# State part's products in parts of 64 output partitions, with the order of a group's work rearranged

## What is computed

```python
scores = einsum('bclhg,bcshg->bchls', Cc, Bc) * decay * dtT
Y_intra = einsum('bchls,bcshp->bclhp', scores, Xc)
w = exp(cum[:, :, -1:, :] - cum) * dtc
S = einsum('bcshg,bcshp->bchgp', Bc * w[..., None], Xc)
carry = dl[:, :, None, None] * carry + s              # state from chunk to chunk
Y_inter = einsum('bclhg,bchgp->bclhp', Cc * exp(cum)[..., None], Hprev)
y = rmsnorm((Y_intra + Y_inter + D_skip[:, None] * Xc) * silu(z), gnorm_w)
# feed-forward part, after the output product, a layernorm and the residual:
scores_xy, idx_xy = top_k(sim, 8)                     # best keys of 2 x 4 heads
w = silu((h . down_embed[chosen]) * softmax(scores))
out = silu(h @ W_up.T) @ W_down.T + sum(w * up_embed[chosen])
```

## Time and profile before

| | |
|---|---|
| runs | 2712.41, 2712.59, 2716.40 us |
| profiled execution | 2715.71 us, span of its trace 2714.0 us |
| busy: PE / DVE / POOL / ACT | 2644.7 / 2252.2 / 2132.0 / 1737.1 us |
| share of the span | 97% / 83% / 79% / 64% |
| mean granted TensorE clock | 0.992 of full |
| one pass in the loop | 81.67 us, the same in every pass to within 0.05 us |

### The profile page before, as it was taken

One profiled execution on the slowest core, in us unless ns is written; L12 is line 12 of the kernel. 1 busy time (PEld: TensorE's weight loads), 2 busy tenths in 40 slices (PEclk: granted clock), 3 DMA queues, 4 the chain that ended last, 5 costly groups with the idle time before them and its releaser, 6 DMA issues. The chain is left out here.

```text
span 2714.0 us, 50697 instructions
## 1 busy us (share of the span) xinstructions
PE 2644.7 (97%) x14888; PEld 2187.2 (81%) x14888; DVE 2252.2 (83%) x5390; ACT 1737.1 (64%) x3687; POOL 2132.0 (79%) x3127
## 2 busy tenths in 40 slices
PE   6899999999999999999999999999999999999988
PEld 5788887888888888887888887888887888887867
DVE  4688888898888898888988888988888888888864
ACT  5566666666666666666666666675666676666643
POOL 4478788888788888788888788888788888888863
PEclk8999999999999999999999999999999999999989
DMA  3000000000000000000000000000000000000000
GB/s 139 9 8 13 13 4 8 12 12 12 12 0 12 12 12 12 8 4 12 12 12 12 8 4 12 12 12 12 5 7 12 12 12 12 4 8 12 8 5 8
DMA packets 28856, 34.26 MB, mean 13 GB/s; under 512 B 2704, under 2 KB 27280, under 8 KB 28240
## 3 DMA queue, kind: packets, MB, share of 16 engines
q1 hardware_dynamic: 28816, 33.77, 3.9%
HBM read 25.37 MB, written 8.39 MB: 12 GB/s over the span
## 5 line engine op out<-in xcount | busy, mean ns | idle before, releaser
L1183 DVE SCALAR_TENSOR_TENSOR acc<-bank,cw,acc 128x253 f32<-128x253 f32 x1920 | 767.9, 471 | 168.4 <-ACT acc L834 168.3
L1539 PE MATMUL bank<-hT,w_in 128*128 128x256 f32 x2560 | 603.1, 381 | 8.7 <-DVE acc L1183 7.9
L1539 PEld LDWEIGHTS bank<-hT,w_in 128*128 128x128 f32 x2560 | 482.6, 191 | 114.2 <-issue 45.2
L642 POOL TENSOR_TENSOR Em<-ee 128x1024 f32<-128x1024 f32 x256 | 558.5, 2201 | 7.6 <-issue 7.6
L1338 DVE SCALAR_TENSOR_TENSOR Em<-Em,p 128x1024 f32<-128x1024 f32 x256 | 418.0, 1643 | 4.9 <-POOL Em L642 4.9
L969 ACT ACTIVATE Em<-Em,rden 128x1024 f32<-128x1024 f32 x256 | 292.6, 1144 | 139.2 <-DVE Em L1347 139.2
L834 ACT ACTIVATE acc<-bank,cb,cw 128x253 f32<-128x253 f32 x640 | 323.7, 559 | 0.0
L657 POOL TENSOR_TENSOR W<-W,Em 128x1024 f32<-128x1024 f32 x122 | 315.1, 2583 | 7.7 <-POOL ee L627 0.2
L1347 DVE TENSOR_TENSOR Em<-Em,products 128x1024 f32<-128x1024 f32 x252 | 305.4, 1212 | 3.3
L1725 PE MATMUL bank<-h2T,w_up 128*128 128x256 f32 x1024 | 242.1, 379 | 1.4 <-ACT hid L947 1.4
L1759 PE MATMUL bank<-w_ue,WT 128*128 128x256 f32 x1024 | 236.2, 384 | 4.9 <-ACT WT L979 4.9
(11 more groups left out here) (208 smaller groups left out, 5240.7 us busy)
## 6 DMA issues: line engine op xcount, KB each, us to landing
x_in<-x_dram SPq DMA_DIRECT2D x32, 256.0 KB, 2.7
x_res<-x_dram SPq DMA_DIRECT2D x32, 256.0 KB, 2.7
out_dram<-f SPq DMA_DIRECT2D x32, 256.0 KB, 2.2
w_in<-in_wT_dram SPq DMA_DIRECT2D x1, 1544.0 KB, 8.8
w_in<-in_wT_dram SPq DMA_DIRECT2D x1, 1024.0 KB, 5.2
w_up<-upT_dram SPq DMA_DIRECT2D x1, 1024.0 KB, 13.4
w_de<-down_eT_dram SPq DMA_DIRECT2D x1, 1024.0 KB, 15.4
w_down<-downT_dram SPq DMA_DIRECT2D x1, 1024.0 KB, 17.4
```

The source lines that it names most:

```text
L642: nc.gpsimd.tensor_tensor(Em[:, k], bc(ee[:, k, 0:XD], 2, KEYS), bc(ee[:, k, XD:XD + KEYS], 1, XD), ALU.mult).then_inc(E_done.sem, 1)
L1183: ins = V.scalar_tensor_tensor(acc[:, r, a, TAPS - 1:], ps[:, a * TOK + k:(a + 1) * TOK - TAPS + 1 + k], cw[:, t, k:k + 1], acc[:, r, a, T ...
L1539: last = mm(ring[j % 2][:, a * TOK:(a + 1) * TOK], w_in[:, k, at:at + P], hT[:, k, :], start=k == 0, stop=k == DK - 1)
```

## The change

The products of `mixer_Yi`, `mixer_S` and the intra-chunk part of `mixer_Yn` are issued as two products each, one for output partitions 0 to 63 and one for 64 to 127; `mixer_dt` is issued in four parts of 32. The number of f32 products in such a block goes from 8 to 16 (dt: 4 to 16) with the same streamed columns. Four waits are added (`mixer_parts` on `cum_sb`, `mixer_state` on `ecum_done`, `ffn_times` on `A_ps`, `ffn_A` on `h2T_sb`), and every engine's order is rearranged. These steps move from the end of a pass to the start of the next: on POOL `weigh(., 1, 0)`, `tail_root3`, `collect(., 0, 1)`; on ACT `mixer_square(., 1)`, `ffn_experts(., 0, 2)`; on DVE `ffn_times(., 0, 2)` and `(., 0, 3)`, `tail_sum`, `mixer_step(., 1)`. The same steps stand at the head of each engine's `ending`.

Indentation is cut; "..." marks what is left out. First TensorE:

```diff
@@ -1516,8 +1548,9 @@
         pe.wait_ge(Yn_read.sem, Yn_read.at(g - 1, CH - 1))
     for c in range(CH):
         for k in range(DK):
-            last = mm(yb[:, c * HEADS:(c + 1) * HEADS], hT[:, k, c * P:(c + 1) * P],
-                      w_in[:, k, INNER + XBC:], start=k == 0, stop=k == DK - 1)
+            for t in range(0, P, 32):
+                last = mm(yb[t:t + 32, c * HEADS:(c + 1) * HEADS], hT[:, k, c * P + t:c * P + t + 32],
+                          w_in[:, k, INNER + XBC:], start=k == 0, stop=k == DK - 1)
...
     for h in range(HEADS):
-        last = mm(ring[1 - c][:, h * HD:(h + 1) * HD],
-                  xbcT[:, INNER // P + HEADS + h, c * P:(c + 1) * P], H[:, h * HD:(h + 1) * HD],
-                  start=True, stop=True)
+        for t in (0, HALF):
+            last = mm(ring[1 - c][t:t + HALF, h * HD:(h + 1) * HD],
+                      xbcT[:, INNER // P + HEADS + h, c * P + t:c * P + t + HALF],
+                      H[:, h * HD:(h + 1) * HD], start=True, stop=True)
     last.then_inc(Yi_ps.sem, 1)
...
     pe.wait_ge(X_sb.sem, X_sb.at(g, c))
     for h in range(HEADS):
-        last = mm(ring[c][:, h * HD:(h + 1) * HD], Btok[:, h, :], Xw[:, h * HD:(h + 1) * HD],
-                  start=True, stop=True)
+        for n in (0, HALF):
+            last = mm(ring[c][n:n + HALF, h * HD:(h + 1) * HD], Btok[:, h, n:n + HALF],
+                      Xw[:, h * HD:(h + 1) * HD], start=True, stop=True)
     last.then_inc(S_ps.sem, 1)
 
...
     pe.wait_ge(sL_done.sem, sL_done.at(g, 2 * c + 1))
     for h in range(HEADS):
-        last = mm(yb[:, h * HD:(h + 1) * HD], sL[:, h, :], Xdt[:, h * HD:(h + 1) * HD],
-                  start=False, stop=h == HEADS - 1)
+        for t in (0, HALF):
+            last = mm(yb[t:t + HALF, h * HD:(h + 1) * HD], sL[:, h, t:t + HALF],
+                      Xdt[:, h * HD:(h + 1) * HD], start=False, stop=h == HEADS - 1)
     last.then_inc(Yn_ps.sem, 1)
 
```

In the orders below the lines `if a:`, `if b:`, `if c:` and the like (is there a group g, e, f) are left out. TensorE's order, to `mixer_out`:

```diff
+pe.wait_ge(folded, 4)
+mixer_dt(g)
 pe.wait_ge(folded, 2)
-pairs(0, 1)
-pe.wait_ge(folded, 4)
-mixer_dt(g)
+mixer_pair(g, 0)
+ffn_down(f, 0)
+mixer_pair(g, 1)
+mixer_pair(g, 2)
 ffn_A(f, 1)
-pairs(2)
-ffn_down(f, 0)
-pairs(3)
+mixer_pair(g, 3)
 tail_h2T(e, g)
 pe.wait_ge(folded, 6)
 mixer_z(g, 0)
+ffn_sim(e, 0)
 mixer_z(g, 1)
 search_weights()
-ffn_sim(e, 0)
-pairs(4)
+mixer_pair(g, 4)
+mixer_pair(g, 5)
 ffn_sim(e, 1)
-pairs(5)
+ffn_WT(f, 0, f if e is None else e)
 ffn_up(e, 0)
-ffn_WT(f, 0, f if e is None else e)
-pairs(6)
+mixer_pair(g, 6)
 ffn_up(e, 1)
-pairs(7)
+mixer_pair(g, 7)
+mixer_cum(g, e)
+mixer_pair(g, 8)
+ffn_up(e, 2, g)
 ffn_out(f, 0)
-mixer_cum(g, e)
-pairs(8)
-ffn_up(e, 2, g)
-pairs(9)
 ffn_up(e, 3)
+mixer_pair(g, 9)
 ffn_WT(f, 1, None)
 ffn_A(e, 0)
+mixer_rows(g, 0, f)
 mixer_X(g, 0)
-mixer_rows(g, 0, f)
 ffn_out(f, 1)
+mixer_Yi(g, 0)
 mixer_B(g, 0)
-mixer_Yi(g, 0)
+mixer_scores(g, 0)
+mixer_X(g, 1)
 mixer_hT(n, e)
-mixer_scores(g, 0)
-mixer_X(g, 1)
+mixer_S(g, 0)
 mixer_rows(g, 1, f)
 mixer_Yn(g, 0, e, n)
-mixer_S(g, 0)
 mixer_B(g, 1)
 mixer_scores(g, 1)
 mixer_Yi(g, 1)
+mixer_Yn(g, 1, e, n)
 mixer_yT(g, 0)
-mixer_Yn(g, 1, e, n)
 mixer_S(g, 1)
 mixer_yT(g, 1)
 mixer_out(g, 0)
```

ACT's:

```diff
-pairs(0, 1)
+mixer_square(e, 1)
+ffn_experts(f, 0, 2)
+mixer_dt(g)
+mixer_pair(g, 0)
+ffn_experts(f, 0, 3)
 tail_keep(f)
-ffn_experts(f, 0, 3)
-mixer_dt(g)
-pairs(2)
+mixer_pair(g, 1)
+silu(g, 0)
+mixer_pair(g, 2)
+tail_norm(e, g)
+tail_h2T(e)
 mixer_u(g)
-tail_norm(e, g)
-pairs(3)
-tail_h2T(e)
 mixer_dt_exp(g)
+silu(g, 1)
+mixer_pair(g, 3)
+ffn_sim(e, 0)
 mixer_z(g, 0)
 mixer_z(g, 1)
 search_weights()
-ffn_sim(e, 0)
+silu(g, 2)
+mixer_pair(g, 4)
+silu(g, 3)
+mixer_pair(g, 5)
+ffn_sim(e, 1)
 ffn_experts(f, 1, 0)
-pairs(4)
-ffn_sim(e, 1)
+ffn_WT(f, 0)
+ffn_up(e, 0)
+silu(g, 4)
+mixer_pair(g, 6)
 ffn_experts(f, 1, 1)
-pairs(5)
+ffn_up(e, 1)
+mixer_cum(g)
 ffn_experts(f, 1, 2)
-ffn_up(e, 0)
-ffn_WT(f, 0)
-pairs(6)
+silu(g, 5)
+mixer_pair(g, 7)
+silu(g, 6)
+mixer_pair(g, 8)
+ffn_up(e, 2)
 ffn_experts(f, 1, 3)
-ffn_up(e, 1)
-pairs(7)
-mixer_cum(g)
-pairs(8)
-ffn_up(e, 2)
-pairs(9)
+silu(g, 7)
+mixer_pair(g, 9)
+ffn_WT(f, 1)
+ffn_exp(e)
 ffn_up(e, 3)
+silu_head(g)
 silu(g, PAIRS - 2)
-silu_head(g)
+mixer_move(g, 0)
+mixer_norm(n, e)
 silu(g, PAIRS - 1)
-ffn_WT(f, 1)
-mixer_move(g, 0)
-ffn_exp(e)
 mixer_exp(g)
 mixer_decay(g, 0)
-mixer_norm(n, e)
 mixer_B(g, 0)
 mixer_hT(n)
+mixer_decay(g, 1)
+mixer_B(g, 1)
 mixer_move(g, 1)
-mixer_decay(g, 1)
-mixer_B(g, 1)
+ffn_norm(f)
 mixer_square(g, 0)
 ffn_experts(e, 0, 0)
 ffn_experts(e, 0, 1)
 mixer_yT(g, 1)
-mixer_square(g, 1)
-ffn_norm(f)
-ffn_experts(e, 0, 2)
```

DVE's:

```diff
-conv(0)
+ffn_times(f, 0, 2)
+ffn_times(f, 0, 3)
+tail_sum(e)
+mixer_step(e, 1)
+mixer_conv(g, 0)
+ffn_mask(f, 1, 0)
 tail_residual(e)
-conv(1)
+mixer_conv(g, 1)
 fold(loaded_z, 0, INNER)
+mixer_conv(g, 2)
+ffn_mask(f, 1, 1)
+mixer_conv(g, 3)
+ffn_times(f, 1, 0)
+ffn_times(f, 1, 1)
 ffn_last(f, 1)
-ffn_mask(f, 1, 0)
-conv(2, 3)
-ffn_times(f, 1, 0)
-for h in range(1, RH):
-ffn_mask(f, 1, h)
-ffn_times(f, 1, h)
-conv(4, 5, 6)
+ffn_mask(f, 1, 2)
+ffn_times(f, 1, 2)
+mixer_conv(g, 4)
 ffn_best(e, 0)
-conv(7, 8, 9)
-fold_out()
+ffn_mask(f, 1, 3)
+mixer_conv(g, 5)
+mixer_conv(g, 6)
+ffn_times(f, 1, 3)
+mixer_conv(g, 7)
+mixer_conv(g, 8)
 ffn_best(e, 1)
 mixer_stats(n)
+mixer_conv(g, 9)
+fold_out()
 ffn_choose(e)
+ffn_stats(f)
 mixer_state(g, 0)
+ffn_last(e, 0)
 mixer_scores(g, 0)
-ffn_last(e, 0)
-ffn_mask(e, 0, 0)
+ffn_mask(e, 0, 0, 1)
+mixer_step(g, 0)
 mixer_gate(g, 0)
-ffn_stats(f)
-mixer_step(g, 0)
 ffn_times(e, 0, 0)
 mixer_scores(g, 1)
-ffn_mask(e, 0, 1)
 mixer_state(g, 1)
 ffn_times(e, 0, 1)
 mixer_gate(g, 1)
-mixer_step(g, 1)
-ffn_mask(e, 0, 2)
-ffn_mask(e, 0, 3)
+ffn_mask(e, 0, 2, 3)
 ffn_store(f)
-ffn_times(e, 0, 2)
-tail_sum(g)
-ffn_times(e, 0, 3)
 dve.wait_ge(own_dve, own.n)
```

POOL's:

```diff
+weigh(f, 1, 0)
 mixer_dt_abs(g)
+weigh(f, 1, 1)
+tail_root3(e)
 tail_root4(e)
-weigh(f, 1, 1, 2, 3)
+weigh(f, 1, 2)
+collect(f, 0, 1)
+weigh(f, 1, 3)
 collect(f, 0, 2, 3)
 mixer_dt(g)
+collect(f, 1, 1)
+mixer_parts(g)
 mixer_keep(g)
-collect(f, 1, 1, 2, 3)
-mixer_cum(g)
-mixer_parts(g)
+collect(f, 1, 2, 3)
 ffn_args(e, 0)
+ffn_args(e, 1)
 mixer_head(g)
-ffn_args(e, 1)
 mixer_norm(n)
+mixer_cum(g)
+mixer_scale(g, 0)
+weigh(e, 0, 0, 1)
+mixer_decay(g, 0)
 mixer_halo(n)
+weigh(e, 0, 2)
+ffn_root(f)
+mixer_scale(g, 1)
+weigh(e, 0, 3)
+mixer_root_y(g)
 pool.wait_ge(rden_done.sem, rden_done.at(e))
-mixer_scale(g, 0)
-weigh(e, 0, 0)
-mixer_decay(g, 0)
-weigh(e, 0, 1, 2, 3)
-mixer_scale(g, 1)
 mixer_decay(g, 1)
-ffn_root(f)
-mixer_root_y(g)
-weigh(e, 1, 0)
-tail_root3(g)
-collect(e, 0, 1)
```

More of the change, by code:

```diff
@@ L23 @@
 CHUNK = 128
+HALF = 64
 CH = 2
@@ L1070, in do_group @@
                 if a:
+                    silu(g, PAIRS - 1)
+                    mixer_exp(g)
+                    mixer_decay(g, 0)
                     mixer_B(g, 0)
@@ L1398, in do_group @@
                     mixer_stats(n)
+                if a:
+                    mixer_conv(g, 9)
+                if a and not later(g):
+                    fold_out()
                 if b:
                     ffn_choose(e)
-                if a:
-                    mixer_state(g, 0)
-                    mixer_scores(g, 0)
-                if b:
-                    ffn_last(e, 0)
-                    ffn_mask(e, 0, 0)
-                if a:
-                    mixer_gate(g, 0)
                 if c:
@@ L1411, in do_group @@
                 if a:
+                    mixer_state(g, 0)
+                if b:
+                    ffn_last(e, 0)
+                if a:
+                    mixer_scores(g, 0)
+                if b:
+                    ffn_mask(e, 0, 0, 1)
+                if a:
                     mixer_step(g, 0)
+                    mixer_gate(g, 0)
                 if b:
@@ L1764, in do_group @@
                 a, b, c = g is not None, e is not None, f is not None
-                def pairs(*js):
-                    for j in js:
-                        if a:
-                            mixer_pair(g, j)
-                if a and not later(g):
-                    pe.wait_ge(folded, 2)
-                pairs(0, 1)
                 if a and not later(g):
@@ L1777, in do_group @@
                     mixer_dt(g)
+                if a and not later(g):
+                    pe.wait_ge(folded, 2)
+                if a:
+                    mixer_pair(g, 0)
+                if c:
+                    ffn_down(f, 0)
+                if a:
+                    mixer_pair(g, 1)
+                    mixer_pair(g, 2)
                 if c:
                     ffn_A(f, 1)
-                pairs(2)
-                if c:
-                    ffn_down(f, 0)
-                pairs(3)
+                if a:
+                    mixer_pair(g, 3)
                 if b:
```

114 lines of the change are left out of this document (59 added, 55 removed).

## The result

The changed kernel takes **2802.7 us** (median of 4 runs, 2800.75 to 2807.88) against 2712.5 us: a ratio of 1.0332, 95% interval 1.0314 to 1.0350. It is 3.3% slower, and outside the range of the prediction.

What follows compares the result with a forecast made beforehand. TensorE's gapless stream was taken as the bound. Blocks -3.07, dt 0 and waits +2.05 gave -1.0 us a pass, counted 31 times: 2715.7 to 2685 us, less 3.1 for the median, 2682 us; range 2600 to 2755.

Steps and rivals of the forecast that it cites:

- What bounds the kernel: Loop pass of 81.67 us: 80.8 us gapless TensorE stream plus 0.84 us of waits; VectorE next, 11.5 us below.
- The split products: Six TensorE blocks a pass: halves run beside each other, 0.94 us a block in place of 1.75, before switching costs.
- The switch of form: TensorE entering and leaving smaller tiles: 0.30 us a block, making it 1.24 us; six blocks then save 3.07 us a pass.
- dt: mixer_dt in 32 records, sets of four, plus a switch: between 0.54 and 1.26 us, taken as 0.82, no change.
- Pair 3: ScalarE starts pair 3 later, behind other steps and two table loads: new TensorE wait of 1.6 us before z of chunk 1.
- Pairs 4 to 7: After convolution 3, VectorE's 13.0 to 13.5 us of work against TensorE's 13.0: wait of 0 to 0.5 us, taken as 0.3.
- End of the pass: Two more ScalarE table loads before the decay, partly covered: waits between 0 and 2.6 us, taken as 1.0.
- The moved steps: Steps moved to the start of a pass, and added waits: no cost; if cover is gone, up to 1 us.
- the order costs more than the split gives: Rival: slower masks put VectorE behind from convolution 0 to 7, waits 5.1 us, +1.2 us a pass, 2750 us; chance 0.20.
- No overlap: Rival: split halves run one behind the other, a pair taking 0.11 us, some 3 us more a pass, 2805 us; chance 0.07.
- the sum of waits: TensorE's waits a pass under the new order: 1.6 + 0.3 + 1.0 = 2.9 us in place of 0.84, 2.05 us more.

Runs made afterwards that it cites:

- after_p3_z: Changed kernel with ScalarE's silu(1) and pair 3 start ahead of tail_h2T, mixer_u and mixer_dt_exp, and both chunks' z ahead of ffn_sim on TensorE and ScalarE: 2687.9 us.

## Why the prediction was wrong

*What bounds the kernel*: right. TensorE's stream was the time, and what counts is which waits an order leaves.

*The split products*: right. Halves run beside each other: 32 records in 1.08 us, 16 pairs of 60 ns and 0.12 us around them. The row of L1493 carried over from 64 contraction rows to 128.

*The switch of form*: right in size. Between full-size work a block pays 0.12 us in itself (1.08 for 16 pairs), 0.09 in the block ahead and 0.05 in the block behind, together 0.26 where I had taken 0.30; so it costs 1.22 us for my 1.24. The Trainium skill's page TensorEngine Tiling (Array Packing), section Key Properties, says that a change of mode drains the engine, and the 0.09 us by which the block ahead lengthens agree with that. The price is too small to speak against the change: a block still gains 0.5 us.

*dt*: I took no change between 0.54 and 1.26 us; it is 0.36, with its neighbours 0.48, below my lower end.

Together the stream fell by 3.5 us a pass for my 3.07, and nearly all of that difference is dt.

*Pair 3*: the step was right and 0.5 us short: 2.1 for 1.6. The chain from the end of pair 3 on TensorE (1284.08) to the end of its convolution is 9.3 us against my 8.93, and TensorE reached z of chunk 1 after the 7.33 us counted. What I had at nothing is the clock: I held waits to cost their own length, and behind this one it falls in 20 of 27 passes, for 1.7 us each, 1.3 us a pass on average. I had also not looked at the next users of z's banks; the wait of 1.2 us before pair 4 costs nothing as long as TensorE stands for pair 3, and shows once that is mended. Both edits together (`after_p3_z`) give back 115 us. The kernel then takes 2687.9 us, close to the forecast of 2682, but by chance: the wait of 1.6 us that the forecast contains is gone from it, and the end of the pass costs 2.5 us more than forecast.

*Pairs 4 to 7*: 0.3 us expected; 0.2 us was found, at `ffn_up`, `ffn_WT` and pair 4.

*End of the pass*: the mechanism (two more table loads) was right and the size not. For chunk 0, X waits 1.5 us, Yi 0.3 and B 0.6: 2.4 where I took 1.0, though inside my bounds of 0 and 2.6. For chunk 1 I had let the waits vanish behind longer cover, without a reason that holds: `mixer_B` there still holds 1.34 us for 0.87, as before, and S, the transposes of y and what is behind them wait another 0.6. The covers that I counted are themselves the split blocks, each 0.7 us shorter. Together 3.5 us for 1.0.

*The moved steps*: at nothing, and nothing shows against it: the list has no wait for the steps that moved to the start of a pass.

*The rivals*: "the order costs more than the split gives" is what happened, at 2803 instead of 2750 us, but not in its place: the masks were not late, VectorE stood idle for 5 us in front of convolution 3. The point from which it decides, 3.9 us of waits a pass, was passed at 5.9, without the clock. "No overlap", which gave 2805 us, is refuted although its number fits: the blocks hold 1.08 us.

The step that failed is the sum of waits, 2.9 us a pass in place of 0.84. The runs show 5.9 us, of which 3.5 stand at the end of the pass (1.0 forecast) and 2.1 at pair 3 (1.6 forecast), and on top the slow clock, 1.3 us a pass on average, which had no term. With the stream at -3.5 that is -3.5 + 5.9 - 0.84 + 1.3 = +2.9 us a pass, as measured (81.67 to 84.5), where the forecast had -1.0. That the pair 3 wait and its clock are the larger part of the loss is shown by an edit. The wait before X is shown in ScalarE's rows, but no edit turned it into time; the exact share of each other wait at the end of a pass stays open, as each edit there moved ScalarE's table loads elsewhere.

## What to carry to other kernels

On a kernel whose bound engine runs without gaps, cutting that engine's work and rearranging all orders are two changes: time them apart. The cut was worth 2.2% and the new orders cost 5.1% (3.3% together: in the new orders the cut is worth 2.3 us in a pass with the full clock, but with it the clock falls far more often). When a step moves ahead of a hand-off, add up everything on the other engine between the hand-off and its use, table loads first, and check the next users of the same bank too, since one wait can hide another. A wait on TensorE can cost more than its length. And price a changed block by its neighbours as well as by itself.

## What was not expected of the hardware

- Products with 64 streamed columns hold TensorE as long as those with 128 (108 to 112 ns a record), at 128 weight columns; in halves of 64 output partitions two take 60 ns, and sets of four parts of 32 with 8 columns 45 ns each, taken over the whole block of dt (0.36 us).
- Going into the smaller form and back costs about 0.26 us a block between full-size blocks: 0.12 in the block, 0.09 in the block ahead, 0.05 in the one behind.
- Behind a wait of 2.1 us, with 3.5 us around it in which TensorE was busy 1.57 us, the clock was granted at half its rate for part of the next 7 us, at a price of 1.7 us, in 20 of 27 passes; behind the same wait in the kernel without the splits in 3 of 27. What decides it is open.
- Where an order alternates Exp and Silu, ScalarE loads a table each time, 1.28 us: six loads a pass against four before.
- The same multiplication of two tiles of 128x512 on VectorE took 0.69, 0.95 and 1.51 us, the longer the more of it lay beside one step of GpSimd.
